# A finer order within a step: TensorE's dense work and VectorE's other work in pieces between the attention units

## The reference: what is computed

```python
mod = (silu(c) @ wmod).reshape(8, 6, 1, -1)        # sa, ca, ga, sb, cb, gb; ga, gb kept away from 0
h = layernorm(x) * (1 + ca) + sa
q, k, v = split(h @ w_in.T)                        # 16 heads of 16 channels
att = softmax(causal(q @ k.T / 4)) @ v
x = x + ga * (att @ w_out.T + b_out)
h = layernorm(x) * (1 + cb) + sb
xr = mu_r * h + (1 - mu_r) * h_prev                # h_prev: h of the token before
xk = mu_k * h + (1 - mu_k) * h_prev
x = x + gb * sigmoid(xr @ W_r.T) * (relu(xk @ W_k.T) ** 2 @ W_v.T)
```

## Time and profile before

| | |
|---|---|
| median of three runs | 1754.11 us (1753.4 to 1755.41) |
| span of the profiled execution, first to last instruction | 1747.5 us |
| the profiled execution's own time | not listed by itself; the runs lie 5.9 to 7.9 us over its span |
| busy share: TensorE, VectorE, ScalarE, GpSimd | 84%, 67%, 52%, 42% |
| TensorE's weight loads | 44% |
| mean granted TensorE clock | 0.930 of full speed |

### The profile page before, as it was taken

The page is one execution under the profiler, slowest core; times in us unless marked ns, Lnnn a source line. Parts: engine busy times, 40 slices in busy tenths (PEclk is TensorE's granted clock), DMA queues, the critical chain, the costliest instruction groups (busy, mean ns, idle before and its releaser), DMA issues.

```text
span 1747.5 us, 33032 instructions
## 1 busy us (share of the span) xinstructions
PE 1460.0 (84%) x10024; PEld 767.3 (44%) x10024; DVE 1176.4 (67%) x2307; ACT 911.6 (52%) x1795; POOL 731.7 (42%) x876
## 2 busy tenths in 40 slices
PE   2599999889897888879888898978889799889754
PEld 2343435444543445444444445434454344544344
DVE  4368677867677775767767775787757777677232
ACT  1146555555565554555555554555545655555622
POOL 2213213445344443544334553344434443444555
PEclk8679999899998999999998999989999999999966
DMA  3111113111311113111221113111131111211200
GB/s 103 38 64 57 45 57 100 44 50 55 99 56 35 56 57 97 57 42 51 74 79 41 54 56 95 58 39 54 53 94 66 39 51 65 67 56 44 60 28 18
DMA packets 101873, 102.98 MB, mean 59 GB/s; under 512 B 21296, under 2 KB 89912, under 8 KB 101696
## 3 DMA queue, kind: packets, MB, share of 16 engines
q1 hardware_dynamic: 99136, 92.38, 16.3%
q0 software_dynamic: 2560, 8.39, 1.3%
HBM read 31.74 MB, written 8.94 MB: 23 GB/s over the span
## 4 chain that ended last, share of the span: by engine, by line
PE 49%; DVE 21%; issue 12%; ACT 9%; POOL 6%; SPq 2%; DMA 1%; DVEq 1%; ACTq 0%; POOLq 0%
PE row_ps L1058 9%; PE val_ps L1082 9%; PE col_ps L1028 7%; PE dense_ps L1092 7%; DVE max_a L855 6%; PE dense_ps L1093 5%; PE dense_ps L1094 5%; ACT weights L699 4%; DVE mixed L968 2%; DVE max_b L855 2%; PE row_ps L1063 2%; PE dense_ps L1111 2%; SPq L457 2%; DVE xn_c L894 1%; DVE gated L952 1%
## 5 line engine op out<-in xcount | busy, mean ns | idle before, releaser
L699 ACT ACTIVATE weights<-col_ps 128x512 f32<-128x512 f32 (+1 forms) x1216 | 621.0, 580 | 475.3 <-PE col_ps L1028 473.4
L855 DVE TENSOR_REDUCE max_a<-row_ps 128x1 f32<-128x512 f32 (+3 forms) x864 | 550.1, 663 | 249.1 <-PE row_ps L1063 162.1
L1058 PE MATMUL row_ps<-k_stack,q_stack 96*128 96x512 bf16 (+3 forms) x1536 | 470.8, 345 | 52.6 <-DVE max_a L855 32.4
L1028 PE MATMUL col_ps<-q_stack,k_stack 99*128 99x512 bf16 (+3 forms) x1536 | 400.2, 337 | 52.2 <-ACT weights L699 32.3
L590 POOL TENSOR_SCALAR_AFFINE_SELECT weights<-weights 128x512 f32<-128x512 f32 x256 | 170.1, 664 | 557.9 <-ACT weights L699 555.9
L1082 PE MATMUL val_ps<-weights,v_ones 128*32 128x512 f32 (+3 forms) x3072 | 336.5, 511 | 15.5 <-POOL weights L590 15.2
L1058 PEld LDWEIGHTS row_ps<-k_stack,q_stack 96*128 96x128 bf16 x1536 | 147.4, 100 | 353.9 <-DVE max_a L855 166.8
L855 DVE TENSOR_REDUCE max_b<-row_ps 128x1 f32<-128x384 f32 (+3 forms) x352 | 213.2, 635 | 120.4 <-PE row_ps L1063 120.1
L1028 PEld LDWEIGHTS col_ps<-q_stack,k_stack 99*128 99x128 bf16 x1536 | 133.9, 99 | 219.8 <-ACT weights L699 136.8
L1063 PE MATMUL row_ps<-causal,ident_bf 128*128 128x128 bf16 x1024 | 208.5, 228 | 0.0
L1063 PEld LDWEIGHTS row_ps<-causal,ident_bf 128*128 128x128 bf16 x1024 | 104.9, 102 | 15.0 <-issue 0.7
(11 more groups left out here) (128 smaller groups left out, 2290.0 us busy)
## 6 DMA issues: line engine op xcount, KB each, us to landing
q_stack<-q_part SPq DMA_DIRECT2D x384, 64.0 KB, 2.6
k_stack<-k_part SPq DMA_DIRECT2D x384, 64.0 KB, 2.6
xa<-in_x SPq DMA_DIRECT2D x8, 1024.0 KB, 6.4
att<-val_out SPq DMA_DIRECT2D x64, 128.0 KB
recips<-recip_rows SPq DMA_DIRECT2D x32, 256.0 KB
xq<-in_x SPq DMA_DIRECT2D x28, 256.0 KB, 3.2
out<-xq POOLq DMA_DIRECT2D x28, 256.0 KB, 2.6
q_stack<-max_rows SPq DMA_DIRECT2D x192, 4.0 KB
```

The lines of the kernel that those rows point to most:

```text
L699: nc.scalar.activation(weights[:, t % 2, h:h + n, 0:q1 - q0], col_ps[bank][:, 0:n * (q1 - q0)].rearrange("p (h q) -> p h q", h=n), ACT.Exp ...
L855: nc.vector.reduce_max(dest, bank[:, 0:len(heads) * (k1 - k0)].rearrange("p (h k) -> p h k", h=len(heads)), AX_X).then_inc(max_done, 1)
L1028: last = nc.tensor.matmul(col_ps[bank][:, i * (q1 - q0):(i + 1) * (q1 - q0)], k_stack[s % 2][:, h, P * j:P * (j + 1)], q_stack[s % 2][:, h ...
L1058: last = nc.tensor.matmul(bank[:, n * width:(n + 1) * width], q_stack[stack][0:ROWS, h, P * i:P * (i + 1)], k_stack[stack][0:ROWS, h, k0:k ...
```

## The change

- **TensorE**: after each score unit come its share of the step's row units and its share of the dense unit, which is cut into pieces (`PIECES`: four of three matmuls; q and k three of two; transposes stay whole). Values come after all of that. In step 0 no rows stand between the score units. Where a step has two dense units (group 0, steps 1 and 2) the second stays whole at the end, after values.
- **VectorE**: what reads the dense bank (`gated`, `mix_out`) comes first in the step (`back_evacuate`), and the other work is cut into pieces, one after each maximum. Before the last maximum, what is left of the pieces and `rest_of_qk` are done.
- **ScalarE**: what reads the dense bank (h, recept, `k_relu`) comes first in the step, before the exponentials; `k_sq` and `k_hi` stay in the middle of them.
- **Steps**: norm moves from `u` = 5 to 6, recept from 9 to 10, key from 10 to 11; out stays at 2 and value at 13. Their consumers and the chains between move too: h and its difference to 7, mixing to 8, `mix_hi` and `mix_lo` to 9, `k_relu`, `k_sq`, `k_hi` and `k_lo` to 12 (step 0 of the next group). One qk unit moves from step 6 to 5, and the front's transposes from 4, 6, 8, 10 to 3, 5, 7, 9.

No matmul, activation or copy is added or removed; some semaphores count in finer units.

```diff
--- before.py
+++ after.py
@@ -83,10 +83,11 @@
 assert sum(PER_STEP) == len(ORDER)
-V_STEPS, QK_STEPS, T_STEPS = (0, 1, 2, 3), (4, 6, 7, 8), (4, 6, 8, 10)
+V_STEPS, QK_STEPS, T_STEPS = (0, 1, 2, 3), (4, 5, 7, 8), (3, 5, 7, 9)
 BACK_UNITS = ("out", "norm", "recept", "key", "value")
-BACK_STEPS = dict(zip(BACK_UNITS, (2, 5, 9, 10, 13)))
+BACK_STEPS = dict(zip(BACK_UNITS, (2, 6, 10, 11, 13)))
 BACK_END = 15
 TAIL_LAG = 5
...
@@ -632,10 +625,10 @@
                                             ALU.subtract).then_inc(o_lo_done, 1)
                 if u == 4:
                     rstd(var_c, mv_c, rstd_c, mv_c_done, var_c_done, rstd_c_done, q + 1)
-                if u == 6:
+                if u == 7:
...
                     wait(pool, ready["key"], q)
                     for m in range(2):
                         pool.wait_ge(mix_hi_done, q * 2 + (m + 1))
                         nc.gpsimd.tensor_tensor(mix_lo[:, m], mixed[:, m], mix_hi[:, m].bitcast(F32),
                                                 ALU.subtract).then_inc(mix_lo_done, 1)
-                if u == 11:
+                if u == 12:
                     pool.wait_ge(k_hi_done, q + 1)
                     nc.gpsimd.tensor_tensor(k_lo[:], k_sq[:], k_hi[:].bitcast(F32), ALU.subtract
                                             ).then_inc(k_lo_done, 1)
...
                     last.then_inc(free["transposed"], 1)
-            def back(b, s, u):
+            def back_evacuate(b, s, u):
                 q = quarters(b, s)
...
                         last = nc.scalar.activation(h2[s % 2][:, c, 1:1 + QT], dense_ps[:, c, :], ACT.Identity,
                                                     bias=mod_back[:, c:c + 1], scale=mod_back[:, 2 + c:3 + c])
                     last.then_inc(free["norm"], 1)
-                if u == 8:
+                if u == 11:
+                    act.wait_ge(ready["recept"], q + 1)
+                    wait(act, free["value"], q)
+                    nc.scalar.activation(recept[:], dense_ps[:], ACT.Tanh, scale=0.5).then_inc(free["recept"], 1)
+                if u == 12:
+                    act.wait_ge(ready["key"], q + 1)
...
+            def back(b, s, u):
+                q = quarters(b, s)
+                if u == 1:
+                    act.wait_ge(att_done, b * 2 - (1 if s < 2 else 0))
+                    wait(act, ready["out"], q)
+                    nc.scalar.activation(o_hi[:], att_n[:, :, QT * s:QT * (s + 1)], ACT.Copy).then_inc(o_hi_done, 1)
+                if u == 9:
...
@@ -779,6 +777,8 @@
             def body(b, kind):
                 for s, t, at in timeline(b, kind):
                     units = range(COL_FIRST[t], COL_FIRST[t + 1]) if attends(kind) else ()
+                    for item in at:
+                        back_evacuate(*item)
                     for c in units[:len(units) // 2]:
                         exps(b, s, t, c)
...
+            def back_evacuate(b, s, u):
+                q = quarters(b, s)
+                if u == 3:
+                    dve.wait_ge(ready["out"], q + 1)
+                    ga = gates_att[:, 0:1, :].broadcast_to([P, 2, D])
+                    nc.vector.tensor_tensor(gated[:], dense_ps[:], ga, ALU.mult).then_inc(free["out"], 1)
+                if u == 14:
+                    dve.wait_ge(ready["value"], q + 1)
+                    wait(dve, out_done, q)
+                    nc.vector.scalar_tensor_tensor(mix_out[:], recept[:], 1.0, dense_ps[:], ALU.add, ALU.mult
+                                                   ).then_inc(free["value"], 1)
...
+                    yield
                 if u == 0 and s == 0:
                     nc.vector.tensor_copy(mod_back[:], mod_t[:, bass.ds(b * 8 - 4, 4)]).then_inc(mod_c_done, 1)
                 if u == 3:
-                    dve.wait_ge(ready["out"], q + 1)
-                    ga = gates_att[:, 0:1, :].broadcast_to([P, 2, D])
-                    nc.vector.tensor_tensor(gated[:], dense_ps[:], ga, ALU.mult).then_inc(free["out"], 1)
...
+            def pieces_of(b, kind, s, t, at):
+                for item in at:
+                    yield from back(*item)
+                yield from front(b, kind, s, t)
             def body(b, kind):
                 for s, t, at in timeline(b, kind):
-                    units = gaps(t) if has_rows(kind, s) else [[]] * 5
+                    units = range(sum(PER_STEP[:t]), sum(PER_STEP[:t + 1])) if has_rows(kind, s) else ()
+                    pieces = pieces_of(b, kind, s, t, at)
+                    for item in at:
+                        back_evacuate(*item)
                     if t == 0 and attends(kind):
                         maximum(b, s - 1, MT1)
-                    for u in units[0]:
+                    for n, u in enumerate(units):
                         maximum(b, s, u)
-                    for item in at:
-                        back(*item)
-                    front(b, kind, s, t)
-                    for u in units[1] + units[2] + units[3]:
-                        maximum(b, s, u)
-                    rest_of_qk(b, kind, s, t)
-                    for u in units[4]:
-                        maximum(b, s, u)
+                        next(pieces, None)
+                        if n == len(units) - 2:
+                            for _ in pieces:
+                                pass
+                            rest_of_qk(b, kind, s, t)
+                    for _ in pieces:
+                        pass
+                    if len(units) < 2:
+                        rest_of_qk(b, kind, s, t)
...
+            def product(dst, a_hi, a_lo, b_hi, b_lo, done=None, wide=False):
                 for c in range(KC):
                     nc.tensor.matmul(dst, a_hi(c), b_hi(c), start=(c == 0), stop=False)
+                    if wide and c == 1:
+                        yield
                     nc.tensor.matmul(dst, a_hi(c), b_lo(c), start=False, stop=False)
+                    if wide and c == 0:
+                        yield
                     last = nc.tensor.matmul(dst, a_lo(c), b_hi(c), start=False, stop=(c == KC - 1))
-                return last
+                    if done and c == KC - 1:
+                        last.then_inc(done, 1)
+                    if not wide:
+                        yield
...
+            PIECES = {"v": 4, "qk": 3, "transposed": 1, "out": 4, "norm": 1, "recept": 4, "key": 4, "value": 4}
...
+                def dense_pieces(unit, backs_now):
+                    if unit:
+                        claim_dense()
+                        yield from front(unit)
+                    for item in backs_now:
+                        claim_dense()
+                        yield from back(*item)
...
-                    work = (4 * cols + 4 * has_values + 6 * bool(unit) + 6 * len(backs_now)) or 1
-                    rows = iter(range(sum(PER_STEP[:t]), sum(PER_STEP[:t + 1])) if has_rows(kind, s) else ())
-                    total, state = (PER_STEP[t] if has_rows(kind, s) else 0), [0, 0]
-                    def rows_after(amount):
-                        state[0] += amount
-                        while state[1] < min(total, (total * state[0] + work // 2) // work):
-                            row_unit(b, s, next(rows))
-                            state[1] += 1
-                    for c in range(COL_FIRST[t], COL_FIRST[t + 1]) if cols else ():
-                        score_columns(b, s, t, c)
+                    dense = dense_pieces(unit, backs_now)
+                    n_dense = PIECES[unit[0]] if unit else PIECES[back_unit(*backs_now[0])[0]] if backs_now else 0
+                    rows = list(range(sum(PER_STEP[:t]), sum(PER_STEP[:t + 1]))) if has_rows(kind, s) else []
+                    units = list(range(COL_FIRST[t], COL_FIRST[t + 1])) if cols else []
+                    n_rows, n_units = len(rows), len(units)
+                    for k in range(n_units):
+                        score_columns(b, s, t, units[k])
                         if t:
-                            rows_after(COL_HEADS[t])
+                            for u in rows[n_rows * k // n_units:n_rows * (k + 1) // n_units]:
+                                row_unit(b, s, u)
+                        for _ in range(n_dense * k // n_units, n_dense * (k + 1) // n_units):
+                            next(dense)
                     if t == 0 and cols:
                         row_unit(b, s - 1, MT1)
-                        rows_after(4)
+                    if t == 0 or not n_units:
+                        for u in rows[:n_rows - n_rows // 2]:
+                            row_unit(b, s, u)
                     if has_values:
                         values(*late)
-                        rows_after(4)
-                    if unit:
-                        claim_dense()
-                        front(unit)
-                        rows_after(6)
-                    for item in backs_now:
-                        claim_dense()
-                        back(*item)
```

(7 more changed lines are left out.)

121 lines of the change are left out of this document (50 added, 71 removed).

## The result

The changed kernel takes 1899.61 us (median of four runs, 1896.24 to 1906.34) against 1753.76 us (1749.28 to 1755.41) for the kernel before on the same chip: ratio 1.084, 95% interval 1.0813 to 1.0869. The forecast was 1784 us, so the direction was right, the loss of 146 us is five times the 30 us expected, and the time lies outside the range.

A forecast was written before the change was run, and what follows sets the result against it. TensorE's order was taken to set the time, with VectorE nearly bounding the middle windows. A mid batch: -10 + 9.3 + 2 + 3 = +4.3 us; together +30 us on the 1747.5 us span, median 1784 us, range 1762 to 1825.

The forecast's parts named there:

- Part 1, the middle windows: Steps 3 to 8 of each group: VectorE's pieces between maxima gain 10 us a batch, bounds 0 and 15.
- Part 2, the three waits: TensorE waits for GpSimd's `k_lo`, `o_lo`, `mix_lo` before value, out, recept: 8.7 + 6.4 + 8.9 = 24 us a batch.
- Against them stand the idle parts of the outer windows now: Steps 0 to 2 and 9 to 11: present idle time set against the new waits, leaving net loss 9.3 us a batch.
- `rest_of_qk` for `q_part` with a maximum behind it: Sign of being wrong: VectorE's pieces wait in turn, so its idle time in the middle windows does not fall; no size.
- Part 3, the clock: TensorE's waits bring two more costly half-clock stretches a batch, 3 us; bounds 0 and 8.
- The rival in which the clock turns against the kernel: Each of ten waits costs a lower-clock stretch, 10 to 12 us a batch, 1840 us and more; chance 0.07.
- Part 3, the pieces' starts: 39 more dense-piece starts after a bf16 matmul on TensorE, 0.05 us each: 2 us a batch.
- Batches 0 and 7, and the drain: Batch 0 gains 8 us, batch 7 loses about 12, the drain costs nothing, bounds 5 us either way.
- The finer order wins: Rival: new waits sum to less than 19 us a batch, so the kernel takes 1696 to 1730 us; chance 0.36.

The follow-up runs named there:

- Experiment 10: Changed kernel with GpSimd's `select` last in its step, plus VectorE's other work again in one block after the first maximum: 1775.63 us.
- experiment 12: Changed kernel with GpSimd's `select` moved behind the splitting of q and k in step 8 alone: 1884.27 us.
- Experiment 1: Changed kernel with TensorE reading the high part in place of GpSimd's low part, so not waiting for `k_lo`, `o_lo`, `mix_lo` (timing only): 1712.31 us.
- experiment 4: Changed kernel with GpSimd's `select` moved behind its front and back work of the step: 1725.01 us.
- Experiment 14: Changed kernel with GpSimd's order in each step made back work, then front work, then `select`: 1702.13 us.
- experiment 11: Changed kernel with filler, idle 128-column matmuls ahead of value, out and recept, half as many as in a first filler run: 1861.32 us.

## Why the prediction was right in direction and wrong in size

**Part 1, the middle windows: right.** Forecast -10 us a batch, measured 106.4 to 97.1, -9.3. Experiment 10 shows the cause that was named, VectorE's maxima with one piece between them, for 8.7 us of it.

**Part 2, the three waits: right in place and mechanism, the bare ones too long.** They stand where they were put, in steps 1, 2 and 10, behind `select`. The bare waits, that is the idle time before the instruction alone, are in batch 4 6.9, 4.9 and 3.2 us where the working had 8.7, 6.4 and 8.9: 15.0 us and not 24 (15.5 as the mean of batches 2 to 6). Recept's are short because in groups 0 and 2 TensorE has just stood for a maximum and `mix_lo` has been made in the meantime; in experiment 12, where the wait for a maximum shrinks, they are 2.8 us each there in place of 1.8 and 1.2. Experiment 1, which takes all three away, has outer windows of 52.5 + 49.0 = 101.5 us a batch against 70.4 + 56.2 = 126.6: 25.1 us. So the term is right as a sum, and by luck: the bare waits were taken too long and the clock (below) too cheap, and the two errors cancel.

**The step that failed: "Against them stand the idle parts of the outer windows now".** There the windows after the change were built from a floor of counted columns, "9.4 + 0.4" for steps 0 to 2 and 8.25 with "0.3 left over each" for steps 9 to 11, as if whatever keeps TensorE above its columns would vanish. The outer windows were to rise by 9.3 us a batch and rose by 28.7, from 97.9 to 126.6. Less the waits, the forecast is 61.4 - 15.1 = 46.3 for the first and 45.7 - 8.9 = 36.8 for the last ones, 83.1 us a batch. Experiment 1 shows 52.5 + 49.0 = 101.5 without the waits: the forecast has 18.4 us too little, 6.2 in the first and 12.2 in the last windows. Of these 18.4, 5 had been priced apart (2 for the pieces' starts, 3 for the clock); the other 13.4 are nearly all of the miss of 19.6 - 4.3 = 15.3 us a batch. What it consists of:

- The qk chain, about 4 us a batch: experiment 1 keeps it and has 49.0 in the last windows, experiment 4 does not and has 44.0. Of these 5.0 us, 3.7 lie in groups 0 and 2, where q and k are split; 1.3 lie in group 1, which splits none, and are not explained. The chain showed in the view of group 2 above. The prediction had named its mechanism (`rest_of_qk` for `q_part` with a maximum behind it) as something that could spoil the middle windows, and put no price on it at step 8, where `select` stands ahead of the split.
- The turn of the loop. `k_relu` is now ScalarE's first instruction of the next batch's body, and group 3's last window went from 11.0 us (mean) to between 12.9 and 13.1 in the changed kernel and in experiments 1, 4 and 14. The batches tell the turn's part: the loop runs batches 2 to 6 and so turns behind 2 to 5, not behind 1 and 6. Group 3's last window is longer in the former by 1.9 us in the kernel before (11.4 against 9.5), by 2.9 in the changed one (13.8 against 10.8) and by 3.4 to 3.7 in experiments 1, 4 and 14 (13.6 to 13.8 against 10.1 or 10.2). So the turn costs 1 to 2 us more than it did; that the place of `k_relu` is what makes it dearer is argued, and was not tried.
- What was above the floor before and stayed. Rows 1 could have said this: windows of 11.15 and 11.38 us at full clock, with TensorE busy for 10.7 of them, had no wait to lose. Experiment 14, with the feeding in order, still has 11.8 there.

**Part 3, the clock: right in kind, less than half of its size.** Two more costly stretches, 3 us, were taken. Half clock rose from 16 to 40 us a batch, by 24 (26 unrounded), and experiment 11 shows that some 20 us less of it were worth 5.5 to 6.7. At that rate the whole rise is 7 to 8 us a batch, an estimate; 15.5 and 8, together 23 to 24, are then near the 25.1 of experiment 1. The rival in which the clock turns against the kernel (1840 and more, chance 0.07) had the total nearest to the measured one, with 10 to 12 us a batch for the clock, more than the 7 to 8 found. The clock is not the cause by itself: with the filler the kernel still takes 1861 us.

**Part 3, the pieces' starts.** 2 us a batch were taken and 8 by the rule of the Trainium skill ("TensorE: Matmul & The Clock Gate", section "Weight-path perf modes"). No run isolates them. Experiments 1 and 14 keep every piece and every such load and are faster than before, which fits a small price and does not exclude either number.

**Batches 0 and 7, and the drain.** Batch 0 was to gain 8 us and gained 0.8. Its qk units and their chain are the same, and with experiment 14's order it takes 158.4 us, 4.2 less than before: half of the forecast. Batch 7 lost 21.6 (12 forecast) by the same waits: those for the three low parts are 15.6 us there, 1.8 before. The drain, costed at nothing with 5 us either way, lost 13.5 together with batch 7's last three steps, and experiment 14 keeps 11.4 of it. TensorE's waits for GpSimd's low parts in that stretch, first in the kernel before (1643.5 to 1747.5):

```profile
PE dense_ps L1092 <- POOL o_lo L631: 16.5, 3, 5.8
PE dense_ps L1092 <- POOL k_lo L656: 4.2, 2, 3.3
PE dense_ps L1092 <- POOL mix_lo L652: 3.0, 3, 1.5
```

and in the changed one (1781.7 to 1899.2), where `o_lo` has 1.3 us left:

```profile
PE dense_ps L1112 <- POOL mix_lo L645: 25.2, 5, 6.4
PE dense_ps L1112 <- POOL k_lo L649: 9.4, 3, 3.6
```

They rose from 23.7 to 35.9 us, 12.2 of the 13.5, and experiment 1, whose TensorE waits for no low part, takes 99.5 us there, 4.5 less than the kernel before. The drain has no attention and so no `select`, and GpSimd's order cures little in it (115.4 us in experiment 14). Which of the moved steps makes `mix_lo` late there was not tried.

**The rivals.** "The finer order wins" needed the waits below 19 us. They were, at 15.5, and it lost all the same, since its threshold rested on the same floor. Its own price of 1696 to 1730 us came true only when GpSimd's order was changed too (1702 and 1725).

What stays open: which moved step the drain's loss comes from, what the half clock costs that the filler did not take away, what group 1's 1.3 us in the last windows are, and why the first windows of groups 2 and 3 stay 1.4 to 2.4 us above their 9.4 us of columns even in the fastest kernels (10.8 to 11.8).

## What to carry to other kernels

When an instruction on one engine is moved earlier, walk the in-order queue of each engine that feeds it: here three small GpSimd operations and a split stood behind one instruction that waits for everything, and their order in the queue alone was worth 197 us. Cost an edit against the window as it was measured, not against a floor of counted work; an idle part without a named wait is not there to be won. Where stalls of 1 to 3 us appear on TensorE, add to each what it does to the clock. Look at the drain by itself: it has its own waits, and a cure in the steady part need not reach it.
